# Gathers that carry an explicit index bound and skip what lies beyond it: a graph-attention layer on one core

## The chip, the core and the metric

The kernel runs on one core of one Trainium2 chip. The core has five engines with instruction streams of their own: TensorE (PE, matmuls), VectorE (DVE), ScalarE (ACT), GpSimd (POOL) and SyncE (SP). SP and ACT issue plain DMAs, POOL issues the indirect ones (gathers and scatters by a list of indices). The metric is the device time of one execution in microseconds (us).

## What is computed

A graph-attention layer with 12,500 nodes, 212,500 edges sorted by destination, 128 features and 8 heads of 16. After a layer norm and a ReLU of x:

```python
q = (node_h @ Wq.T + bq).reshape(N, 8, 16)
k = (edge_h @ Wk.T + bk).reshape(-1, 8, 16)
v = (node_h @ Wv.T + bv).reshape(N, 8, 16)
qs, qd = (q[src], q[dst])
in_m = jnp.sum(qs * k, axis=-1)
out_m = jnp.sum(qd * k, axis=-1)
diag_m = jnp.sum(qs * qd, axis=-1)
att = jnp.power(distance, lam)
score = (_segment_softmax(in_m * SCALE, dst, N) + _segment_softmax(out_m * SCALE, dst, N)
         + _segment_softmax(diag_m * SCALE, dst, N)) * att
h = jax.ops.segment_sum(score[..., None] * v[dst], dst, num_segments=N)
out = leaky_relu(h.reshape(N, 128) @ Wo.T + bo, 0.1)        # and x + out is returned
```

`q[src]` has no order: the sources of 128 neighbouring edges lie anywhere in the query table. `q[dst]` is sorted.

## The kernel before

The program is written engine by engine, with every wait given by hand as a semaphore and a count. It has three passes.

**Node pass.** It works through 98 tiles of 128 nodes and writes the query table `q_tab` and the value table `v_tab` to DRAM. `q_tab` has 12,672 rows of 128 floats: NPAD = 12,544 rows for the nodes (12,500 padded up) and 128 rows of zeros behind them. Meanwhile POOL fetches rows of the destination list with `fetch_rows` (line 141, 77 of its 99 gathers here).

**Edge pass.** The edges, padded to 212,992, are cut into 1,664 tiles of 128. A unit is 16 tiles, a group is 4, so there are 104 units and 416 groups. For each group

- SP loads four windows of `q_tab` for the destinations (`window`), and for each unit the source indices (`idx_sb`, one column of 128 indices for each tile) and some smaller tables;
- ACT loads the edge features (`ea_sb`);
- POOL fetches the source rows: `fetch_sources` issues four indirect DMAs (line 150), one for each tile. Each takes 128 indices, one for each partition, and lands 128 rows of 512 bytes in `qsrc`, a ring of 8 groups. Before a group POOL waits until PE has turned the group that lay in the ring's slot 8 groups earlier (`qs_turned`, through `need`, line 69), and adds one to a semaphore of its own (line 766);
- PE makes the keys (`k_ps`, line 811), the destination queries (`qd_ps`, line 822), turns the source rows (`qs_ps`, line 831), and sums the products by head (`lg_ps`, line 802); DVE forms the products (`prod`, lines 1015 and 1019), masks and running sums; ACT copies out of PSUM.

POOL's own part of this pass is short:

```python
def unit(h, q):
    u = QUAD * h + q
    pool.wait_ge(idx_in[q], 16 * (h + 1))
    for g in range(NG):
        need(pool, qs_turned, NG * u + g - RING + 1)
        pool.sem_inc(pool_turns, 1)
        fetch_sources(pool, q, g)
```

Four units are written out, 24 times four run in a loop, and four are written out again. Behind them POOL fetches the last 22 rows of destinations (line 141) and mends one result row for each partition with a gather and a scatter on `state` (lines 778 and 782).

**Output pass.** 98 gathers (line 159) fetch the last result row of each node from `state`; the engines divide, sum, project and store.

No gather of the kernel before names a bound; all carry the default by which an index out of range is an error.

Of the kernel before, what the change touches and what calls it, by code (L numbers as in the profile page):

```python
# [31 lines left out]
NPAD = P * NT  # L32
# [7 lines left out]
GRP = 4  # L40
# [25 lines left out]
def need(eng, sem, n):  # L66

    if not isinstance(n, int) or n > 0:
        eng.wait_ge(sem, n)


def gnn_kernel(nc, x, idx, dst_rows, dst_prev, dst_first, tile_first, ea, dist, wqvT, bqv, wkT, bk, woT, bo, lam,
# [12 lines left out]
    with ExitStack() as ctx:  # L85
        def sb(name, shape, dt=F32):
            return ctx.enter_context(nc.sbuf_tensor(name, shape, dt))

        def sem(name):
            return ctx.enter_context(nc.semaphore(name))  # L90


        ident = sb("ident", [P, P])
        wk_sb = sb("wk_sb", [P, F])
        bk_col = sb("bk_col", [P, 1])
        heads = sb("heads", [P, NG, 2 * SUP])
        node_col = sb("node_col", [P, 1])
        nid = sb("nid", [P, NCOL + 1])
        tile_f = sb("tile_f", [P, NN])
        cnt = sb("cnt", [P, NN])  # L100
        qsrc = sb("qsrc", [P, RING, GRP, F])
        q_in = [sem(f"q_in{r}") for r in range(RING)]
        rows_i = sb("rows_i", [P, NBUF, LB * P], I32)
        st = rows_i[:, 0:2, :].rearrange("p b n -> p (b n)").bitcast(F32)[:, 0:RST * HALF * ROW].rearrange(
            "p (r t k) -> p r t k", r=RST, t=HALF)
        st_in = [sem(f"st_in{r}") for r in range(RST)]
        le = sb("le", [P, LB, P])
        idx_sb = sb("idx_sb", [P, QUAD, SUP], I32)
        idx_in = [sem(f"idx_in{q}") for q in range(QUAD)]
        rows_in = [sem(f"rows_in{r}") for r in range(NBUF)]  # L110
        rows_used = sem("rows_used")
        rows_turns = sem("rows_turns")
        bases_in = sem("bases_in")
        q_out = [sem("q_out0"), sem("q_out1")]
        zeros_out = sem("zeros_out")
        tile_i = sb("tile_i", [P, NN], I32)
        le_ready = sem("le_ready")
        bases = sb("bases", [1, T], I32)
        last_i = sb("last_i", [P, NT + 1], I32)
        has = sb("has", [P, NT])  # L120
        fix_i = sb("fix_i", [P, 1], I32)
        whole_pen = sb("whole_pen", [P, 1])
        cont_pen = sb("cont_pen", [P, 1])

        def count(dve, m):

            dve.wait_ge(rows_in[BUF[m]], 16 * LB * (BUF[:m].count(BUF[m]) + 1))
            need(dve, rows_used, m)
            nc.vector.tensor_tensor(le[:, :, :], rows_i[:, BUF[m], :].rearrange("p (l i) -> p l i", i=P),
                                    nid[:, m * LB:(m + 1) * LB].unsqueeze(2).to_broadcast([P, LB, P]), ALU.is_le  # L130
                                    ).then_inc(le_ready, 1)
            dve.wait_ge(le_ready, m + 1)
            nc.vector.tensor_reduce(cnt[:, m * LB:(m + 1) * LB], le[:, :, :], AX_X, ALU.add).then_inc(rows_used, 1)

        def fetch_rows(pool, m, tile_i):

            if BUF[m] in BUF[:m]:
                pool.wait_ge(rows_used, max(k for k in range(m) if BUF[k] == BUF[m]) + 1)
            pool.sem_inc(rows_turns, 1)
            for j in range(LB):  # L140
                pool.indirect_dma_start(out=rows_i[:, BUF[m], j * P:(j + 1) * P], out_offset=None, in_=dst_rows,  # L141
                                        in_offset=bass.IndirectOffsetOnAxis(
                                            ap=tile_i[:, m * LB + j:m * LB + j + 1], axis=0)
                                        ).then_inc(rows_in[BUF[m]], 16)

        def fetch_sources(pool, q, g):

            for j in range(GRP):
                r = (NG * q + g) % RING
                pool.indirect_dma_start(out=qsrc[:, r, j, :], out_offset=None, in_=q_tab,  # L150
                                        in_offset=bass.IndirectOffsetOnAxis(
                                            ap=idx_sb[:, q, g * GRP + j:g * GRP + j + 1], axis=0)
                                        ).then_inc(q_in[r], 16)

        def fetch_results(pool, k):

            for j in range(WIDE[k]):
                at = FROM[k] + j + 1
                pool.indirect_dma_start(out=st[:, k % RST, j, :], out_offset=None, in_=state,  # L159
                                        in_offset=bass.IndirectOffsetOnAxis(ap=last_i[:, at:at + 1], axis=0)  # L160
                                        ).then_inc(st_in[k % RST], 16)

        block = ctx.enter_context(nc.Block())

        nodes_done = node_pass(nc, locals())
        edges_done = edge_pass(nc, locals())
        out_pass(nc, locals())
# [1303 lines left out]
```

## Time and profile before

| | us |
|---|---|
| median of 3 runs | 3120.44 |
| lowest and highest run | 3106.76, 3139.47 |
| profiled execution, first to last instruction (span) | 2381.5 |
| POOL, PE, DVE, ACT busy in the span | 1776.3, 1795.2, 1750.2, 932.8 |

The page states no other time of the profiled execution than its span, so the 738.9 us between the span and the median are not broken down by any view. A POOL gather's busy time is the time in which POOL makes the transfer, not the time in which the rows travel; "issue" is time in which an engine waited for nothing that the profile shows. Register and semaphore instructions of a sequencer appear as POOLq.

### The profile page before, as it was taken

The page shows a single profiled execution, that of the slowest core. Times are in us where ns is not written, and L with a number is a line of the kernel's source. Part 1 is how long each engine was busy: PE and PEld are TensorE (multiplying, and loading weights), DVE is VectorE, ACT ScalarE, POOL GpSimd, SP SyncE. Part 2 cuts the span into 40 slices and gives each one's busy share as a digit, 9 for nine tenths or more (in the row PEclk, how much of TensorE's full clock was granted, in tenths as well). Part 3 has the DMA queues.
Part 4 walks back from the last instruction along what each step waited for, and adds up shares of the span by engine and source line. Part 5 has one row for each costly group of instructions (what it writes and reads, how often), then busy time and mean ns, then how long its engine had stood idle before and what let it go on. Part 6 is the DMA issues. An engine that isn't in the chain of part 4 may idle for free.

```text
span 2381.5 us, 44129 instructions
## 1 busy us (share of the span) xinstructions
PE 1795.2 (75%) x10768; PEld 1095.8 (46%) x10768; DVE 1750.2 (73%) x2904; ACT 932.8 (39%) x1931; POOL 1776.3 (75%) x1869
## 2 busy tenths in 40 slices
PE   5557887877778878778787877778778777777277
PEld 4434454444444444444454444444444444444155
DVE  7749887777767777777777776777677777677556
ACT  5413444444334444434344443444344344434112
POOL 5777777777777777777777777777777777777675
PEclk9868999898888888888889898888889899889566
DMA  7797887777777778777777777777777777774455
GB/s 263 221 295 220 243 259 229 220 233 223 234 207 235 233 220 233 221 221 232 222 231 224 231 231 219 228 229 228 221 228 231 223 229 226 228 224 127 132 146 169
DMA packets 440885, 527.91 MB, mean 222 GB/s; under 512 B 87325, under 2 KB 306721, under 8 KB 440850
## 3 DMA queue, kind: packets, MB, share of 16 engines
q1 hardware_dynamic: 297858, 227.38, 32.3%
q10 hardware_dynamic: 83376, 180.80, 21.9%
q0 software_dynamic: 59616, 119.35, 20.3%
q8 instruction: 12, 0.20, 0.0%
q14 instruction: 23, 0.19, 0.0%
HBM read 442.67 MB, written 84.57 MB: 221 GB/s over the span
## 4 chain that ended last, share of the span: by engine, by line
POOL 51%; issue 19%; PE 12%; DMA 9%; DVE 7%; ACT 1%; POOLq 1%; ACTq 0%; SPq 0%; DVEq 0%
POOL qsrc L150 46%; DMA qsrc<-q_tab,idx_sb 7%; POOL rows_i L159 4%; PE qd_ps L822 3%; PE k_ps L811 3%; PE qs_ps L831 2%; PE lg_ps L802 2%; DVE prod L1019 1%; PE qv_ps L397 1%; POOL rows_i L141 1%; PE t_ps L842 1%; DVE prod L1015 1%; DVE onehot L1005 1%; ACT hb L337 1%; DMA pa_tab<-pa 0%
## 5 line engine op out<-in xcount | busy, mean ns | idle before, releaser
L150 POOL DMA_INDIRECT qsrc<-q_tab,idx_sb x1664 | 1580.0, 950 | 507.3 <-issue 496.6
L831 PE MATMUL qs_ps<-ident,qsrc 128*128 128x128 f32 x1664 | 294.9, 306 | 379.0 <-DMA qsrc<-q_tab,idx_sb 376.1
L822 PE MATMUL qd_ps<-onehot,window 128*128 128x128 f32 x3328 | 530.0, 310 | 62.4 <-DVE onehot L1005 56.4
L898 ACT COPY kq<-qd_ps 128x512 f32<-128x512 f32 x416 | 242.8, 584 | 841.1 <-PE qd_ps L822 834.5
L1019 DVE TENSOR_TENSOR prod<-qs_ps,kq 128x1024 f32<-128x1024 f32 x416 | 507.0, 1219 | 83.7 <-PE qs_ps L831 80.6
L822 PEld LDWEIGHTS qd_ps<-onehot,window 128*128 128x128 f32 x3328 | 477.7, 221 | 137.7 <-issue 75.9
L811 PE MATMUL k_ps<-ea_sb,wk_sb 128*128 128x512 f32 x832 | 497.6, 684 | 33.5 <-DMA ea_sb<-in_ea 33.5
L1015 DVE SCALAR_TENSOR_TENSOR prod<-k_ps,bk_col,kq 128x512 f32<-128x512 f32 x416 | 309.1, 743 | 286.4 <-PE lg_ps L802 274.7
L831 PEld LDWEIGHTS qs_ps<-ident,qsrc 128*128 128x128 f32 x1664 | 214.3, 158 | 470.6 <-issue 464.2
L802 PE MATMUL lg_ps<-prod,heads 128*32 128x384 f32 x3328 | 360.9, 506 | 0.1
L892 ACT ACTIVATE kq<-k_ps,bk_col 128x512 f32<-128x512 f32 x416 | 285.8, 687 | 184.1 <-PE k_ps L811 155.9
L1005 DVE TENSOR_SCALAR_CACHE_REDUCE onehot<-near_sb,node_col 128x512 f32<-128x512 bf16 x416 | 306.1, 736 | 5.8 <-DMA near_sb<-near_tab 5.8
L842 PEld LDWEIGHTS t_ps<-ident,sums 128*128 128x128 f32 x936 | 118.5, 154 | 229.3 <-issue 224.1
L1051 DVE TENSOR_TENSOR_SCAN sums<-max_ps,terms 128x387 f32<-128x387 f32 x208 | 189.0, 950 | 3.6
L802 PEld LDWEIGHTS lg_ps<-prod,heads 128*32 128x32 f32 x3328 | 66.1, 109 | 268.1 <-issue 166.6
L842 PE MATMUL t_ps<-ident,sums 128*128 128x128 f32 x936 | 179.4, 304 | 6.1 <-DVE sums L1051 4.0
L922 ACT COPY rows<-t_ps 128x384 f32<-128x384 f32 x312 | 149.2, 478 | 76.6 <-PE t_ps L842 65.5
L811 PEld LDWEIGHTS k_ps<-ea_sb,wk_sb 128*128 128x128 f32 x832 | 150.2, 225 | 33.8 <-issue 33.8
L1030 DVE TENSOR_TENSOR_SCAN max_ps<-pa_sb,lg_ps 128x387 f32<-128x387 f32 x104 | 100.5, 966 | 73.1 <-ACT terms L905 66.2
L141 POOL DMA_INDIRECT rows_i<-in_dst_rows,tile_i x99 | 100.2, 1013 | 44.8 <-issue 29.9
L159 POOL DMA_INDIRECT rows_i<-state,last_i x98 | 92.6, 945 | 32.2 <-issue 29.6
L1036 DVE TENSOR_TENSOR diffs<-lg_ps,sums 128x384 f32<-128x384 f32 x104 | 58.1, 558 | 56.9 <-ACT sums L910 56.3
(147 smaller groups left out, 1014.6 us busy)
## 6 DMA issues: line engine op xcount, KB each, us to landing
ea_sb<-in_ea ACTq DMA_DIRECT2D x416, 256.0 KB, 3.4
window<-q_tab SPq DMA_DIRECT2D x1664, 64.0 KB
state<-rows ACTq DMA_DIRECT2D x104, 576.0 KB
near_sb<-near_tab SPq DMA_DIRECT2D x104, 512.0 KB
pa_sb<-pa_tab SPq DMA_DIRECT2D x104, 258.0 KB
qsrc<-q_tab,idx_sb POOLq DMA_INDIRECT x1664
xs<-in_x SPq DMA_DIRECT2D x27, 448.0 KB, 4.8
q_tab<-qs SPq DMA_DIRECT2D x14, 448.0 KB, 2.7
```

Of the source, the lines that this page charges most:

```text
L150: pool.indirect_dma_start(out=qsrc[:, r, j, :], out_offset=None, in_=q_tab, in_offset=bass.IndirectOffsetOnAxis(ap=idx_sb[:, q, g * GRP + ...
L802: t = nc.tensor.matmul(lg_ps[2 * SUP * j:2 * SUP * (j + 1), :, 1:W1], heads[:, g, :], prod[:, m % 2, :, j * P:(j + 1) * P], start=g == 0, ...
L811: nc.tensor.matmul(k_ps[:, m % 2, :], wk_sb[:, :], ea_sb[:, p, g * GRP * P:(g + 1) * GRP * P], start=True, stop=True).then_inc(k_ready, 1)
L822: t = nc.tensor.matmul(qd_ps[:, at], window[:, r, j, :], onehot[:, m % 2, at], start=True, stop=True)
L831: t = nc.tensor.transpose(qs_ps[:, m % 2, j * P:(j + 1) * P], qsrc[:, r, j, :], ident[:, :])
L842: t = nc.tensor.transpose(t_ps[:, a * P:(a + 1) * P], sums[:, b, k, a, 1:W1], ident[:, :])
L892: nc.scalar.activation(kq[:, m % 2, 0, :], k_ps[:, m % 2, :], ACT.Identity, bias=bk_col[:, 0:1]).then_inc(k_copied, 1)
L898: nc.scalar.copy(kq[:, m % 2, 1, :], qd_ps[:, :]).then_inc(qd_copied, 1)
L1005: nc.vector.tensor_scalar(onehot[:, m % 2, :].rearrange("p (j i) -> p j i", j=GRP), near_sb[:, p, :, :].rearrange("p (j g) i -> p g j i", ...
L1015: nc.vector.scalar_tensor_tensor(out=prod[:, g % 2, 2, :], in0=k_ps[:, g % 2, :], scalar=bk_col[:, 0:1], in1=kq[:, g % 2, 1, :], op0=ALU.a ...
L1019: nc.vector.tensor_tensor(prod[:, g % 2, 0:2, :], qs_ps[:, g % 2, :].unsqueeze(1).to_broadcast([P, 2, GRP * P]), kq[:, g % 2, :, :], ALU.m ...
L1051: s = nc.vector.tensor_tensor_scan(sums[:, b, k, :, :].rearrange("p a i -> p (a i)"), max_ps[:, :, :].rearrange("p a i -> p (a i)"), terms ...
```

## The change

Each of the 1,664 gathers of source rows gets an explicit bound, 12,543 (the last row of `q_tab` that belongs to a node slot), and the flag that an index above it is not an error: its row is left unfetched. The other gathers are as they were.

```diff
                 pool.indirect_dma_start(out=qsrc[:, r, j, :], out_offset=None, in_=q_tab,
                                         in_offset=bass.IndirectOffsetOnAxis(
-                                            ap=idx_sb[:, q, g * GRP + j:g * GRP + j + 1], axis=0)
+                                            ap=idx_sb[:, q, g * GRP + j:g * GRP + j + 1], axis=0),
+                                        bounds_check=NPAD - 1, oob_is_err=False
                                         ).then_inc(q_in[r], 16)
```

In the built program the bound is held in a register: ahead of each such gather POOL's stream has one more instruction, a move of the constant 12,543 to a register of its own, and the gather names that register. The order of all other instructions, on POOL and on the other engines, is unchanged.

## Rows read from the trace of the kernel before

**Rows 1.** The page's chain that ended last, by engine and by line.

```profile
POOL 51%; issue 19%; PE 12%; DMA 9%; DVE 7%; ACT 1%; POOLq 1%; ACTq 0%; SPq 0%; DVEq 0%
POOL qsrc L150 46%; DMA qsrc<-q_tab,idx_sb 7%; POOL rows_i L159 4%; PE qd_ps L822 3%; PE k_ps L811 3%; PE qs_ps L831 2%; PE lg_ps L802 2%; DVE prod L1019 1%; PE qv_ps L397 1%; POOL rows_i L141 1%; PE t_ps L842 1%; DVE prod L1015 1%; DVE onehot L1005 1%; ACT hb L337 1%; DMA pa_tab<-pa 0%
```

**Rows 2.** The tile qsrc: its gathers, and who waits.

```profile
engine op xcount: duration ns min/median/max, first and last start us, forms
L150 POOL DMA_INDIRECT qsrc<-q_tab,idx_sb x1664: 940/944/2625, 118.0 to 2204.0; - x185
...
who waited for it (us, times):
  PE qs_ps L831: 376.1, 142
...
  POOL qsrc L150: 10.7, 35
```

**Rows 3.** Groups of POOL instructions: busy, mean ns, idle before them and its releaser.

```profile
line engine op names shapes xcount | busy us, mean ns | idle before us <-releasers
L150 POOL DMA_INDIRECT qsrc<-q_tab,idx_sb x1664 | 1580.0, 950 | 507.3 <-issue 496.6 <-PE qs_ps L831 10.7
L141 POOL DMA_INDIRECT rows_i<-in_dst_rows,tile_i x99 | 100.2, 1013 | 44.8 <-issue 29.9 <-DVE tile_i L460 14.9
L159 POOL DMA_INDIRECT rows_i<-state,last_i x98 | 92.6, 945 | 32.2 <-issue 29.6 <-DVE edge_i L1155 2.7
L782 POOL DMA_INDIRECT state<-fixed,fix_i x1 | 2.1, 2110 | 3.5 <-DVE fixed L1127 3.5
```

**Rows 4.** The chain in order of time, in mid edge pass, across a group's boundary.

```profile
1001.39 0.94 POOL qsrc L150
1002.34 0.30 issue
1002.64 0.94 POOL qsrc L150
1003.59 0.03 issue
1003.61 0.03 POOLq L69
1003.65 0.14 issue
1003.79 0.02 POOLq L766
1003.80 0.09 issue
1003.89 0.94 POOL qsrc L150
1004.84 0.30 issue
```

**Rows 5.** Register instructions of POOL's sequencer at line 69 (ns, first and last start).

```profile
L69 POOLq ALU_OP  x288: 32/32/45, 191.5 to 2104.8; - x144
L69 POOLq FUSED_REGOPS  x96: 46/46/52, 188.7 to 2089.8; - x96
```

**Rows 6.** Busy time of each engine in the loop of the edge pass.

```profile
core 0: us, PE busy (x) PEld busy (x) DVE busy (x) ACT busy (x) POOL busy (x), PEclk, DMA share, GB/s
200.00:2100.00 1900.00, 1495.59 (x9254) 893.53 (x9253) 1433.86 (x2224) 777.45 (x1623) 1437.31 (x1518) 0.89 0.77 227
```

**Rows 7.** PE's waits in that stretch, longest first.

```profile
engine line waited for: us in total, times, longest us
PE qs_ps L831 <- DMA qsrc<-q_tab,idx_sb: 353.0, 133, 6.1
PE qd_ps L822 <- DVE onehot L1005: 44.5, 28, 5.9
PE qs_ps L831 <- DVE prod L1019: 2.5, 1, 2.5
```

## The prediction

> **What bounds the kernel now.** I read the chain of work that ended last first. The gathers of source rows (line 150) are 46% of it, and "issue", time in which an engine waits for nothing that the profile shows, another 19% [rows 1]. PE, the busiest engine by its sum, is only 12% of the chain. The reader should see that one engine, POOL, sets the pace of the whole edge pass, although its share of busy time looks like PE's and DVE's.
>
> The tile view of qsrc says it from the other side. The first gather starts at 118.0 us and the last at 2204.0, and PE waits 376.1 us for gathered rows, while POOL waits 10.7 us for PE to free a slot [rows 2]. So the consumer waits for the producer, and hardly ever the other way round: POOL runs without a break. Its groups add up to the same: 1580.0 us busy and 507.3 us idle before the gathers are 2087.3 us, and the stretch from the first start to the last end is 2204.0 + 0.9 - 118.0 = 2086.9 us [rows 2, 3]. One gather therefore costs 2087 / 1664 = 1.254 us: 0.944 us of making the transfer (the median) and 0.30 us of "issue" behind it. In the chain in order of time this beat is plain: 1001.39, 1002.64, 1003.89 [rows 4].
>
> From this follows the price that everything below uses. Whatever is added to each gather is paid 1,664 times on the path that sets the end: **1 ns for each gather is 1.66 us**. About 1% (31.2 us of 3120.44) is what a measurement of this kernel can tell from no change, and that is 18.8 ns for each gather.
>
> The Trainium skill, "DMA: Bandwidth & Descriptors", section "Anatomy of one DMA — SWDGE (gpsimd) path", has a rule that would make any such addition free: it calls the making of descriptors a small, variable part of a fixed cost of about 2 us, and says that many can be emitted before their cost shows. This trace does not agree for these gathers, since POOL's 0.944 us each stand end to end [rows 4]; by the rule the change would leave the time as it is, by the rows every nanosecond is paid.
>
> **The profiled execution and the median.** The sum is made against the span, 2381.5 us. The median is 738.9 us longer, and no view says where these go. The change touches nothing before the first or behind the last instruction, so I carry them as a constant. If instead all of the kernel's 1,863 indirect DMAs took longer without the profiler, that would be 397 ns each, and the price of an added nanosecond would be the same.
>
> **The change, part by part.**
>
> *What does not change.* The same 1,664 transfers are issued in the same order, with the same indices, rows and landing places. The sources are node numbers up to 12,499 (the padding uses 0) and the bound is 12,543, so no index is ever beyond it and no row is skipped. No wait and no queue moves. SP, ACT, PE and DVE get not one instruction more.
>
> *The move to a register.* 1,664 of them, each just ahead of its gather. No row of the edge pass shows a move on POOL; the nearest are the register operations of line 69, 32 ns for one and 46 ns for a fused one [rows 5]. Exposed, they would give 1664 x 0.032 = 53 us to 1664 x 0.046 = 77 us. But the chain shows what such instructions cost here: at the group's boundary a register operation of 0.03 us, a wait and a semaphore step stand between two gathers, and the next gather starts 1.25 us after the last, as it does inside a group where nothing stands there [rows 4]. They run inside the 0.30 us of "issue" that is there anyway. I take **0**, with 0 to 77 us as the bounds; an added instruction can't give a gain. The cover is that 0.30 us; if it were gone, the 53 to 77 us would be due.
>
> *The bound itself.* This is the open cost: the trace shows no gather with an explicit bound. What it does show is how little a gather's duration depends on what it is told. The gathers of line 150 fetch rows of 512 bytes from 12,672, those of line 159 rows of 288 bytes from 212,992, with a median of 944 ns and a mean of 945 ns [rows 2, 3]. So the duration follows the count of 128 indices, about 0.944 / 128 = 7.4 ns for each, and not bytes or the table's size. From below, a compare that is done in any case, with or without an explicit bound, costs 0. From above, the longest indirect DMA with a form of its own, the single scatter of line 782, took 2110 ns [rows 3]; 1.166 us more each would be 1,940 us. The gather with a bound is the same operation with one parameter more, so it is far nearer to the rows of 944 ns than to the scatter. I take **0**.
>
> *The error flag dropped.* If the report on the indices is made behind each gather, it lies in the 0.30 us of "issue", and dropping it could shorten that. The gain has a floor. In the loop of the edge pass PE waits 353.0 of 1,900 us for gathered rows [rows 6, 7]; take these away and PE, in order and with its other work unchanged, is the bound. That is at most 353.0 / 1900 x 2087 = 388 us. All of the idle time before gathers, 507.3 us, could not be won. No row says that any of it belongs to a report; I take **0**, with 0 to -388 us as the bounds.
>
> *Sum.* 0 + 0 + 0: a span of 2381.5 us, and 2381.5 + 738.9 = 3120.4 us.
>
> **The rivals.**
>
> *A compare for each index (slower).* If POOL makes the explicit bound good index by index, and the compare isn't there before, each of 128 indices gets a step more. With 7.4 ns for an index, and a compare taken as one step in eight (my assumption; one in sixteen to one in four as bounds), that is an estimate of 0.92 ns an index, 118 ns a gather, 1664 x 0.118 = 196 us: **3317 us**, between 3219 and 3513. It decides from 18.8 ns a gather, 0.15 ns an index, on. For it speaks that POOL has no slack at all [rows 2], against it that a gather's duration doesn't move with its parameters [rows 3].
>
> The Trainium skill, "GPSIMD Engine Reference", section "Performance pitfalls for Q7 kernels", gives a body that compares and selects 1.03 to 2.03 cycles for each element; at the 1.2 GHz of its "Specifications" section that is an estimate of 110 to 217 ns for 128 indices, and 183 to 361 us in all. No row here shows such a body.
>
> *The register move is exposed (slower).* If a gather that reads a register can't be prepared until the move is done, the 0.30 us don't cover it: 53 to 77 us, **3185 us** in the middle. Against it stands the unchanged beat at the group's boundary [rows 4], where the wait's count is taken from a register too.
>
> *The report goes away (faster).* If half of the 0.30 us is the report of errors, 1664 x 0.15 = 250 us go: **2870 us**. For it speaks that these 0.30 us are the same behind every gather and nothing recorded fills them [rows 3, 4]; against it, that a report needs an index out of range, and there is none.
>
> *The change does nothing.* If the default already compares with the table's last row, only the number and the reaction change, and the reaction never comes. This is part of the forecast.
>
> **How the numbers follow.** No difference (within 1%): 0.52, at 3120 us. Slower by over 1%: 0.30, made of 0.23 for the compare and 0.07 for the exposed move. Faster by over 1%: 0.18. The predicted time is that of no difference; its own range is the runs' spread and a little, 3100 to 3145 us. The 8-in-10 range must take in part of both sides: up to 3360 us (a compare of 144 ns a gather) it holds the exposed move and about 0.15 of the compare's 0.23; down to 3040 us it holds about a third of the faster case, gains up to 80 us. Left out are about 0.08 above and 0.12 below.
>
> **What would show it.** In the profile of the changed kernel the gathers of line 150 (a line lower) should still have a median of 944 ns and a beat of 1.25 us, with a move on POOL's sequencer inside the 0.30 us of "issue", and PE should wait some 376 us for qsrc. A median above 963 ns shows the compare; a gap of 0.33 us or more with 944 ns unchanged shows the exposed move; a gap well under 0.30 us shows the report gone, and PE's wait for qsrc should then shrink. The prediction is wrong if the gathers' duration depends on the flag in a way that no row of this kernel can show, or if the 738.9 us outside of the span change with it.

## The result, and the profile after

The changed kernel takes 3107.28 us (median of 14 runs, 3088.84 to 3125.11), the kernel before 3131.39 us (14 runs, 3106.76 to 3145.90). The ratio is 0.9938, with a 95% interval of 0.9913 to 0.9963 (it is not the quotient of the two medians, which is 0.9923 and lies inside the interval): no difference by the bound of 1%, but a gain of 0.4 to 0.9% that is clear of noise.

The profile of before that is shown above is of an execution with a span of 2381.5 us, which none of the timed runs of that kernel in this study (3050 to 3146 us) came near, while the same kernel profiled again, as same_again below, has a span of 3058.0 us. The rows of after are therefore set beside those of same_again, and the rows above are named where they answer to them. The long executions' traces also hold fewer semaphore events (20,336 in same_again, 75,900 in that of before, for the same program). So many of their waits have no named releaser ("remote", "another core or an unknown queue"), and a name that is missing there proves nothing; durations and idle times do not hang on it.

The head of the page after, with busy time and the chain of work that ended last [rows 1]:

```profile
span 3107.8 us, 45793 instructions
...
PE 1945.5 (63%) x10768; PEld 1108.8 (36%) x10768; DVE 1740.5 (56%) x2904; ACT 901.6 (29%) x1931; POOL 1856.9 (60%) x1869
...
another core or an unknown queue 40%; PE 18%; DVE 17%; issue 15%; ACT 6%; ACTq 4%; DMA 0%; DVEq 0%; SPq 0%
PE qd_ps L823 6%; DVE prod L1020 5%; PE k_ps L812 4%; PE lg_ps L803 4%; DVE onehot L1006 3%; DVE prod L1016 3%; ACTq L943 2%; PE t_ps L843 1%; ACT kq L899 1%; PE qs_ps L832 1%; ACT kq L893 1%; ACT rows L923 1%; DVE max_ps L1031 1%; DVE diffs L1037 1%
```

The gathers are gone from the chain, where they were 46%. Its largest piece is now time for which the profile knows no releaser, so this chain does not tell what bounds the kernel. The run of this profile took 3109.6 us, so only 1.8 us lie outside of its span.

The groups of POOL instructions after [rows 3], and then the tile qsrc after [rows 2], with what its engines waited for:

```profile
L150 POOL DMA_INDIRECT qsrc<-q_tab,idx_sb x1664 | 1667.2, 1002 | 1004.8 <-issue 487.5 <-remote 281.8 <-PE qs_ps L832 150.9
L141 POOL DMA_INDIRECT rows_i<-in_dst_rows,tile_i x99 | 93.6, 945 | 99.4 <-DVE cnt L133 55.3 <-issue 29.3 <-DVE tile_i L461 14.8
L160 POOL DMA_INDIRECT rows_i<-state,last_i x98 | 92.7, 946 | 64.7 <-DVE ratio L1372 33.5 <-issue 28.6 <-DVE edge_f L1153 2.5
```

```profile
L150 POOL DMA_INDIRECT qsrc<-q_tab,idx_sb x1664: 991/997/2512, 178.9 to 2837.4; - x185
...
who waited for it (us, times):
  POOL qsrc L150: 155.6, 65
  DVE prod L1020: 14.0, 13
```

PE's idle time before the matmuls that need gathered rows, whatever ended it:

```profile
L832 PE MATMUL qs_ps<-ident,qsrc 128*128 128x128 f32 x1664 | 277.9, 289 | 28.4 <-issue 28.2
```

Two things are to be seen. The gathers with a bound have a median of 997 ns instead of 944 (947 in same_again), a minimum of 991 instead of 940, while the gathers without one, lines 141 and 160 in the same execution, have means of 945 and 946 ns (947 both in same_again). And PE hardly waits for gathered rows any more: its idle time before these matmuls is 28.4 us where it waited 376.1 (20.0 us of idle time in same_again). POOL waits for PE 150.9 us by name instead of 10.7. Its idle time before the gathers is 1004.8 us, twice the 507.3 us at which it ran without a break.

POOL's instructions in order of time, in mid edge pass [rows 4], and the added register moves [rows 5]:

```profile
1503.37 1.00 POOL L150 DMA_INDIRECT qsrc<-q_tab,idx_sb  x1 [0.31 <-issue]
1504.67 1.00 POOL L150 DMA_INDIRECT qsrc<-q_tab,idx_sb  x1 [0.30 <-issue]
1508.22 0.99 POOL L150 DMA_INDIRECT qsrc<-q_tab,idx_sb  x1 [2.55 <-PE qs_ps L832]
1509.52 1.22 POOL L150 DMA_INDIRECT qsrc<-q_tab,idx_sb  x1 [0.30 <-issue]
...
1512.35 1.00 POOL L150 DMA_INDIRECT qsrc<-q_tab,idx_sb  x1 [0.30 <-issue]
1513.65 1.00 POOL L150 DMA_INDIRECT qsrc<-q_tab,idx_sb  x1 [0.30 <-issue]
```

```profile
L150 POOLq MOVE  x1664: 29/29/39, 178.1 to 2834.4; - x185
```

The moves are there, 29 ns each, and the gap between two gathers is still 0.30 us. The beat is 1.30 us where it was 1.25, all of it in the gather. Between groups POOL now stops, here for 2.55 us, until PE has freed a slot.

PE's waits after [rows 7] and its loop's busy times [rows 6] complete the picture:

```profile
PE qd_ps L823 <- issue: 387.0, 155, 12.0
PE qd_ps L823 <- DVE onehot L1006: 209.7, 99, 8.7
PE qd_ps L823 <- ACT kq L899: 126.7, 26, 16.5
```

```profile
200.00:2100.00 1900.00, 1267.05 (x7094) 701.58 (x7094) 1099.86 (x1714) 569.80 (x1232) 1188.13 (x1188) 0.83 0.60 179
```

In the same 1,900 us PE does 7,094 matmuls where it did 9,254, and POOL 1,188 transfers where it did 1,518. same_again is like after here:

```profile
200.00:2100.00 1900.00, 1284.49 (x7208) 714.56 (x7208) 1117.74 (x1740) 580.86 (x1253) 1152.32 (x1207) 0.83 0.61 182
```

So this is not the bound's doing. All engines get less done together, and none is full.

### The profile page after: what moved, and what is told of

The parts are those of the page before. It is cut to its first block, busy times and chain, and to the rows that moved or that the text cites. A ratio compares the mean times of both kernels' runs of the same rounds, so it can differ in the third digit from the quotient of the medians.

```text
span 3107.8 us, 45793 instructions
## 1 busy us (share of the span) xinstructions
PE 1945.5 (63%) x10768; PEld 1108.8 (36%) x10768; DVE 1740.5 (56%) x2904; ACT 901.6 (29%) x1931; POOL 1856.9 (60%) x1869
## 4 chain that ended last, share of the span: by engine, by line
another core or an unknown queue 40%; PE 18%; DVE 17%; issue 15%; ACT 6%; ACTq 4%; DMA 0%; DVEq 0%; SPq 0%
PE qd_ps L823 6%; DVE prod L1020 5%; PE k_ps L812 4%; PE lg_ps L803 4%; DVE onehot L1006 3%; DVE prod L1016 3%; ACTq L943 2%; PE t_ps L843 1%; ACT kq L899 1%; PE qs_ps L832 1%; ACT kq L893 1%; ACT rows L923 1%; DVE max_ps L1031 1%; DVE diffs L1037 1%
## 5 line engine op out<-in xcount | busy, mean ns | idle before, releaser
L150 POOL DMA_INDIRECT qsrc<-q_tab,idx_sb x1664 | 1667.2, 1002 | 1004.8 <-issue 487.5
L823 PE MATMUL qd_ps<-onehot,window 128*128 128x128 f32 x3328 | 573.9, 326 | 724.1 <-issue 387.0
L823 PEld LDWEIGHTS qd_ps<-onehot,window 128*128 128x128 f32 x3328 | 495.8, 228 | 867.2 <-issue 632.1
L812 PE MATMUL k_ps<-ea_sb,wk_sb 128*128 128x512 f32 x832 | 538.0, 736 | 32.2 <-DMA ea_sb<-in_ea 32.2
L803 PE MATMUL lg_ps<-prod,heads 128*32 128x384 f32 x3328 | 422.3, 582 | 11.3 <-issue 7.1
L832 PE MATMUL qs_ps<-ident,qsrc 128*128 128x128 f32 x1664 | 277.9, 289 | 28.4 <-issue 28.2
L832 PEld LDWEIGHTS qs_ps<-ident,qsrc 128*128 128x128 f32 x1664 | 207.7, 150 | 112.2 <-issue 110.3
L843 PEld LDWEIGHTS t_ps<-ident,sums 128*128 128x128 f32 x936 | 112.0, 153 | 373.7 <-issue 224.6
L812 PEld LDWEIGHTS k_ps<-ea_sb,wk_sb 128*128 128x128 f32 x832 | 157.0, 235 | 32.6 <-issue 32.6
L141 POOL DMA_INDIRECT rows_i<-in_dst_rows,tile_i x99 | 93.6, 945 | 99.4 <-DVE cnt L133 55.3
```

Of the source, the lines that this page charges most:

```text
L803: t = nc.tensor.matmul(lg_ps[2 * SUP * j:2 * SUP * (j + 1), :, 1:W1], heads[:, g, :], prod[:, m % 2, :, j * P:(j + 1) * P], start=g == 0, ...
L812: nc.tensor.matmul(k_ps[:, m % 2, :], wk_sb[:, :], ea_sb[:, p, g * GRP * P:(g + 1) * GRP * P], start=True, stop=True).then_inc(k_ready, 1)
L823: t = nc.tensor.matmul(qd_ps[:, at], window[:, r, j, :], onehot[:, m % 2, at], start=True, stop=True)
L832: t = nc.tensor.transpose(qs_ps[:, m % 2, j * P:(j + 1) * P], qsrc[:, r, j, :], ident[:, :])
L843: t = nc.tensor.transpose(t_ps[:, a * P:(a + 1) * P], sums[:, b, k, a, 1:W1], ident[:, :])
```

## The experiments

All ratios are to the kernel before, timed beside it on the same chip. There it took 3070 us (the first part below, to extra_step_no_bound), 3079 us (memsets and split windows) and 3078 us (later gathers and one window); beside the change it took 3131 us, so times are compared only within a part. "Gather" is always the median of line 150 (a few lines lower where code was added), in ns.

### The kernel before again, and the change taken apart

**same_again**: the kernel before, no edit.

> The kernel before, unchanged, timed against itself: what a difference of 0.6% is worth, and whether its profile repeats the span of 2381.5 us or comes near the 3131 us of its timed runs. If the 2381.5 us were one odd execution, the span should be 3100 to 3145 us, with gathers of 944 ns, POOL waiting for PE or for its indices, and SP's register instructions stretched to some 700 ns as in the profile after. If the kernel before truly runs at the gathers' pace, the span should be near 2381 us. Ratio 1.000, its interval about 0.3% to either side.

Measured: 3070.0 us, ratio 0.9986 (0.9959 to 1.0013). Its span (below the 3100 us expected, but like the runs beside it), its gathers with the idle time before them, POOL's wait for its indices, and SP's window instructions (minimum, median, maximum in ns), the last line being that of the execution of 2381.5 us:

```profile
span 3058.0 us, 44129 instructions
```

```profile
L150 POOL DMA_INDIRECT qsrc<-q_tab,idx_sb x1664 | 1592.8, 957 | 1025.8 <-issue 459.4 <-remote 274.2 <-PE qs_ps L831 198.3
```

```profile
POOL qsrc L150 <- DMA idx_sb<-in_idx: 82.5, 24, 5.3
```

```profile
L744 SPq FUSED_REGOPS  x1664: 2/37/1397, 201.7 to 2778.2; - x185
L744 SPq MOVE window<-q_tab x1664: 2/29/1397, 201.8 to 2778.3; - x185
```

```profile
L744 SPq MOVE window<-q_tab x1664: 29/29/38, 134.0 to 2166.9; - x185
```

So without the bound, too, POOL waits 1025.8 - 507.3 = 518 us more than its gaps in the execution that the median stands for: for PE, for its indices, and for what no record names. SP's moves to a register, 29 ns at the median, reach 1,397 ns. Against itself the kernel gives an interval that holds 1.000; that of the change, 0.9913 to 0.9963, does not.

**bound_err**: the bound, but an index beyond it is still an error.

```diff
-                                        bounds_check=NPAD - 1, oob_is_err=False
+                                        bounds_check=NPAD - 1
```

> The bound alone: the same 12,543, but an index above it would be reported as an error. If the bound makes the gather longer, its median is 997 ns as after the change, and if the gain hangs on the bound the ratio is 0.992 to 0.996. If the flag is what counts, the gathers stand at 944 ns and the ratio at 1.000.

Measured: 3055.83 us, 0.9932 (0.9908 to 0.9956); gather 1010:

```profile
L150 POOL DMA_INDIRECT qsrc<-q_tab,idx_sb x1664: 1004/1010/2497, 177.5 to 2781.5; - x185
```

```profile
L150 POOL DMA_INDIRECT qsrc<-q_tab,idx_sb x1664 | 1694.0, 1018 | 922.4 <-issue 494.8 <-remote 230.7 <-PE qs_ps L832 152.6
```

The bound makes the gather longer, not the flag; skipping instead of reporting takes 13 ns off again. The gain stands with the bound and without the flag. Beside same_again on the same chip POOL is busy 101 us more (1694.0 against 1592.8) and idle before its gathers 103 us less (922.4 against 1025.8): the longer gathers fit into POOL's waits. That is where the price of the bound went.

**bound_one_register**: bound and flag, with the bound in one register for all gathers.

```diff
+        bound = nc.gpsimd.alloc_register("bound")
...
-                                        bounds_check=NPAD - 1, oob_is_err=False
+                                        bounds_check=bound, oob_is_err=False
...
+            nc.gpsimd.reg_mov(env["bound"], NPAD - 1)
             over_units(pool, unit)
```

> Bound and flag as after the change, but the bound is put in one register once, ahead of all gathers, so the 1,664 moves on POOL are gone. If the gain comes from the longer gather, ratio 0.992 to 0.996 and a median of 997 ns. If it comes from the extra instruction on POOL's sequencer, ratio 1.000.

Measured: 3043.55 us, 0.9895 (0.9862 to 0.9928); gather 997. Without the 1,664 moves the gain is there in full, and by its middle larger. So it does not come from the moves; whether they take 12 us of it back can't be said, since the intervals of this run and the last overlap and the flag differs too.

**extra_step_no_bound**: no bound, but one more instruction on POOL's sequencer.

```diff
                 r = (NG * q + g) % RING
+                pool.sem_inc(bound_steps, 1)
                 pool.indirect_dma_start(out=qsrc[:, r, j, :], out_offset=None, in_=q_tab,
```

> No bound and no flag; instead one more instruction on POOL's sequencer ahead of each gather, an addition of one to a semaphore that nobody waits for. If one more sequencer instruction for each gather is what counts, ratio 0.992 to 0.996 with gathers of 944 ns. If the longer gather counts, ratio 1.000; the gap between gathers should stay at 305 ns in both cases.

Measured: 3094.76 us, 1.0087 (1.0054 to 1.0119); gather 947. Neither of the two ratios expected came: the extra instruction does not help, it costs 0.9%, and that although POOL waits long for others (1064.6 us of idle time before its gathers).

### Does a slower pace of gathers help?

**pace_one_memset** and **pace_three_memsets**: one or three memsets of a column that nobody reads, ahead of each gather (three shown).

```diff
                 r = (NG * q + g) % RING
+                for i in range(3):
+                    nc.gpsimd.memset(pace[:, q, g * GRP + j, i:i + 1], 0.0).then_inc(paced, 1)
...
+                need(pool, env["paced"], 3 * SUP * u)
                 pool.wait_ge(idx_in[q], 16 * (h + 1))
```

> No bound; a memset of one element for each partition stands ahead of each gather on POOL, about 0.1 us, so that the gathers come somewhat later, as they do with the bound. If a slower pace of gathers is what gives the 1%, ratio 0.98 to 0.995. If the gain belongs to the bounded gather itself, the additional instruction only costs: ratio 1.005 to 1.015.

> Three such memsets ahead of each gather, some 0.3 us or more for each. If a slower pace helps, ratio 0.97 to 0.995, unless POOL becomes the bound. If POOL has no slack in the timed runs, the time grows by 1664 times the added time, 300 to 600 us. If it has slack and the pace is of no use, ratio 1.01 to 1.03.

Measured: 3105.71 us, 1.0095 (1.0061 to 1.0128), and 3124.74 us, 1.0141 (1.0076 to 1.0205). Both missed their purpose. POOL in order of time, with three:

```profile
1506.36 0.17 POOL L153 MEMSET pace<- 128x1 f32 x3
1506.68 0.94 POOL L154 DMA_INDIRECT qsrc<-q_tab,idx_sb  x1 [0.15 <-issue]
1507.63 0.17 POOL L153 MEMSET pace<- 128x1 f32 x3
1507.95 0.94 POOL L154 DMA_INDIRECT qsrc<-q_tab,idx_sb  x1 [0.15 <-issue]
```

The memsets run inside the 0.30 us between two gathers; the beat is 1.25 us with one and 1.27 us with three. They hardly changed the pace and only say again what extra_step_no_bound said.

**later_gathers** and **four_groups_ahead**: nothing is added and nothing left out. POOL waits until PE is two, or four, groups further, so the gathers run six, or four, groups ahead instead of eight (shown for six; + 5 gives four).

```diff
-                    need(pool, qs_turned, NG * u + g - RING + 1)
+                    need(pool, qs_turned, NG * u + g - RING + 3)
```

> No bound, no added instruction and nothing left out: before each group POOL waits for PE two groups longer, so the gathers run at most six groups ahead of PE instead of eight. If the 1% of the bounded gathers comes from gathers that are issued later, ratio 0.985 to 0.995. If it belongs to the bounded gather itself, ratio 0.998 or more, up to 1.02 if POOL then makes PE wait.

> As later_gathers, but the gathers run at most four groups ahead of PE. If gathers that are issued later help step by step, the gain grows beyond that of later_gathers: ratio 0.965 to 0.980. If two groups were as much as there is to gain, it stays at 0.980 to 0.987. If PE now waits for gathered rows, ratio 0.99 to 1.03 and PE's wait for qsrc grows from nearly nothing to 100 us or more.

Measured: 3030.23 us, **0.9834** (0.9798 to 0.9870), and 3034.22 us, 0.9861 (0.9817 to 0.9905). The gathers are those of before, and by name they wait longer for PE (198.3 us in same_again; shown for six):

```profile
L150 POOL DMA_INDIRECT qsrc<-q_tab,idx_sb x1664: 938/944/2629, 175.6 to 2764.5; - x185
...
  PE qs_ps L831: 229.7, 101
```

Letting the gathers run fewer groups ahead does help, by more than the bound did and more than the 0.985 to 0.995 expected, and four groups gain no more than six. Why it helps is not shown: POOL's idle time before its gathers, 1013.9 us, is about that of same_again, and the wait for indices is no longer among its named waits. later_gathers is faster than both kernels of this study.

### What holds the timed runs back?

**split_windows** and **split_windows_bound**: two of the four windows of each group (NACT = 2) go to ACT's queue, where load_windows issues them two units ahead; without and with the change.

```diff
-                    for j in range(GRP):
+                    for j in range(GRP - NACT):
                         sp.dma_start(window[:, r, j, :], q_tab[bass.ds(base[j], P), :]).then_inc(window_in[r], 16)
...
+                    if not isinstance(h, int) or QUAD * h + q + 2 < NCOL:
+                        load_windows(QUAD * h + q + 2, slot(q, g)[0], g)
```

> The kernel before, without a bound, but two of the four windows of each group are loaded by ACT's queue instead of SP's, so SP has half as many window instructions. If SP's stretched instructions set the pace of the edge pass and hide POOL, the time falls by several hundred us, down to at best the 2380 us at which the gathers follow one another without a break. If POOL or PE sets the pace, it stays within 1% of 3070.

> The same with the bound and the flag on the 1,664 gathers. If the longer gather is real and was only hidden behind SP, this kernel is slower than split_windows by 1664 times 53 ns, 88 us, as soon as POOL sets the pace there. If the bound helps in itself, it is faster than split_windows by some 0.6% again.

Measured: 3093.75 us, 1.0046 (1.0016 to 1.0077), and 3079.88 us, 0.9979 (0.9939 to 1.0019). With 832 loads taken off SP the kernel is no faster, so the theory that SP's stretched instructions alone set the pace falls; the loads now stand on ACT, which has work of its own in the edge pass, and the next pair leaves them out. The bound gives half a per cent here too, 3079.88 / 3093.75 = 0.9955, though the two intervals overlap.

**one_window** and **one_window_bound**: three of the four windows are not loaded at all; PE counts one load for each group and reads the first window for all four tiles (not shown).

```diff
-                    for j in range(GRP):
+                    for j in range(1):
                         sp.dma_start(window[:, r, j, :], q_tab[bass.ds(base[j], P), :]).then_inc(window_in[r], 16)
```

> Leaves out three of the four window loads of each group (the picks all read the first window, so the destination queries of three tiles in four are not the reference's). No bound. That is 1,248 loads, 160 thousand DMA packets of 512 bytes and about 3,700 instructions of SP fewer; the work of PE, DVE, ACT and POOL is the same. If what holds the timed runs back lies in the traffic of the windows (their packets, or SP's stretched instructions), the time falls by several hundred us, towards the 2380 us at which the gathers follow one another. If it lies in PE, DVE or ACT, it stays near 3080.

> The same left out, with the bound and the flag on the gathers as after the change. If the 53 ns are a real cost of the bounded gather that the slower traffic had hidden, this is slower than one_window by up to 1664 times 53 ns, 88 us, wherever POOL now sets the pace. If the bound is a gain in itself, it is faster than one_window by about 0.6%.

Measured: 3003.25 us, 0.9754 (0.9711 to 0.9798), and 3010.05 us, 0.9773 (0.9729 to 0.9817). Two fifths of the DMA packets gone (261,171 instead of 440,885) give 2.5%, neither the several hundred us nor the 3080 us expected, so the windows' traffic isn't what separates 3070 us from 2381 either. In both kernels POOL still waits for PE, 232.4 us without the bound and 158.4 us with it, so the price of 88 us that the bound would have where POOL sets the pace was not due in any of these kernels and could not be shown. The two differ by 6.8 us with overlapping intervals: the gain of 0.6% that the bound would have in itself does not show here.

## Why the prediction was right, and where its steps were wrong

The forecast, no difference within 1%, is what was measured, and 3107 us lies beside 3120. Three steps behind it did not hold, and two of the signs that it named came out otherwise: the gathers' median is 997 ns and not 944, and PE's wait of some 376 us for qsrc is gone. That the time came out all the same is luck: a cost taken at nothing was real, and the path taken as full had room for it.

**What bounds the kernel.** This is the step that failed: POOL runs without a break, and every nanosecond for each gather is 1.66 us on the path. It was read correctly from the rows, and the rows were of an execution unlike the timed ones. In same_again POOL waits 518 us more than its gaps, PE is idle only 20.0 us before the matmuls that need gathered rows, and in the timed runs 53 ns on each gather cost nothing. The sign was in the table: the span and the median stood 24% apart, and the prediction carried these 738.9 us as a constant outside of the span. The run after shows 1.8 us there. The missing time lies inside the span, in engines that wait: of the 676.5 us between the spans of same_again and before, 520 lie between the first gather and the last, 61 ahead of them and 95 behind.

**The bound itself.** It was taken at 0, because a gather's duration follows neither its bytes nor its table. That is still so for gathers without a bound (945 and 946 ns after the change). But the rival, a compare for each index, was right that the bound makes the gather longer: 997 against 944 ns, 53 ns for 128 indices (50 against same_again). All gathers here have 128 indices, so that the cost goes by the index is not shown; if it does, it is 0.41 ns an index, less than half of the assumed 0.92 and a little under the lower bound (one step in sixteen, 0.46 ns). The estimate of 110 to 217 ns that the prediction worked out from the Trainium skill, "GPSIMD Engine Reference", section "Performance pitfalls for Q7 kernels", was two to four times too high for this gather. Priced as in the prediction it is 88 us and 3208 us; it was not paid because POOL's waits, which the prediction had denied, took it up (bound_err: 101 us more busy, 103 us less idle).

**The register move.** Right: 29 ns each, inside the 0.30 us, the beat's gap unchanged. Not foreseen is that one instruction more for each gather can cost although nobody waits for it: extra_step_no_bound is 0.9% slower with an unchanged gather.

**The error flag.** Taken at 0; it is worth 13 ns a gather, in the gather and not in the 0.30 us gap, which stays. The rival by which the report is half of that gap is out.

**The small gain.** The prediction has no step for it; its terms were costs, or gains of the flag. What is shown: three kernels with the bound are faster than that of before (the change, bound_err, bound_one_register), with the flag and without, with the moves and without. In split_windows the bound's gain of half a per cent is not clear of noise, and in one_window there is none. And gathers that run fewer groups ahead, with nothing else changed, gain 1.7%. That the bounded gather gains for the same reason, because POOL's bursts are slower by 4%, is argued and not shown: a kernel with both was not run, and the memsets that should have slowed the pace alone did not. One semaphore step for each gather moves the time by 0.9% as well, so a difference of this size says little of its cause.

**What stays open** is why the edge pass takes some 2,600 us in the timed runs and 2,087 us in the execution shown ahead. It isn't POOL, which waits, it isn't SP's count of window loads, and only 75 us of it hang on the windows' traffic. The two traces of the same program differ in their count of semaphore events as well, so it is not excluded that how they were recorded is part of the difference; no run here tests it.

The rule of the Trainium skill that the prediction weighed, "DMA: Bandwidth & Descriptors", section "Anatomy of one DMA — SWDGE (gpsimd) path", that descriptors can be made before their cost shows, gave the right time here for another reason: the 53 ns do show in POOL's rows, and are hidden by POOL's own waits.

## What to carry to other kernels

When the span of a profile and the median of the timed runs stand far apart, the profile may not be of what is timed; settle that before a bound is read from it, with a second profile if there is one. An explicit bound on an indirect DMA is a real cost on the engine that makes it, about 5% of a gather of 128 rows here, and was free here because that engine waits for others; what it costs where the engine sets the pace was not shown. A ring that lets a producer run as far ahead as it has slots is not always the best one: here two groups less gave more than the change under study.

## What the runs showed that was not expected

- POOL makes a gather of 128 rows in 944 ns without a bound, 997 ns with a bound that skips, and 1010 ns with a bound that reports; 0.30 us between two gathers take up a register move, a semaphore step or a memset without a longer gap, and three memsets with 0.02 us more.
- In the executions of some 3060 us SP's register instructions reach 1,397 ns where their median is 29 to 37 ns; in the execution of 2381.5 us none of line 744 passes 43 ns. At line 69 of same_again those of SP reach 1,377 ns and those of ACT 700, while none of POOL, DVE or PE passes 60. No run here says what stretches them.
- Eight groups of gathers ahead were slower than six by 1.7%, though PE hardly waited for a gathered row in either (20.0 and 4.9 us of idle time before qs_ps).
